# A two-layer kernel on one core: matmuls that nobody reads in TensorE's pauses, one tile taken ahead of the masking, and mix sums moved from GpSimd to VectorE

## What is computed

```python
xa = _ln(x, ln1_w, ln1_b)
sx = concat([state[:, 1:2] - xa[:, :1], xa[:, :-1] - xa[:, 1:]], axis=1)
xxx = tanh((xa + sx * maa_x) @ maa_w1).reshape(b, l, 5, 32)
xxx = einsum('blfd,fde->blfe', xxx, maa_w2)
xm = xa[:, :, None] + sx[:, :, None] * (maa_stack + xxx)      # five mixes: k, w, v, r, g
...
s = a + w_t * s                                                # the scan over 256 tokens
...
og = group_norm(out) * gn_w + gn_b
x1 = x + og * g @ Wo.T
xc = _ln(x1, ln2_w, ln2_b)                                     # then a channel mix with Wfk, Wfr, Wfv
return x1 + sigmoid(xr2 @ Wfr.T) * (square(relu(xk2 @ Wfk.T)) @ Wfv.T)
```

## Time and profile before

| | us |
|---|---|
| median of three runs | 2015.46 |
| lowest, highest | 2014.08, 2019.63 |
| profiled execution, its own time | 2020.89 |
| span of that execution | 2019.2 |
| TensorE busy | 1889.4 (94%) |
| VectorE busy | 1451.3 (72%) |
| ScalarE busy | 870.1 (43%) |
| GpSimd busy | 471.9 (23%) |
| mean granted TensorE clock | 0.973 |

### The profile page before, as it was taken

How to read it: one execution, slowest core, us unless ns; L and a number is a source line. 1 busy time by engine, 2 the same in 40 slices (tenths; PEclk the granted TensorE clock), 3 DMA queues, 4 the chain that set the end, 5 groups by cost and what they waited for, 6 DMA issues and landing times.

```text
span 2019.2 us, 29336 instructions
## 1 busy us (share of the span) xinstructions
PE 1889.4 (94%) x11284; PEld 1289.5 (64%) x11284; DVE 1451.3 (72%) x2477; ACT 870.1 (43%) x2068; POOL 471.9 (23%) x229
## 2 busy tenths in 40 slices
PE   7899999999999999898899999999999999997587
PEld 5576666666666666566666766767766767656343
DVE  3676766667676634257977898889789789789972
ACT  4577666666667746122243342332432432321222
POOL 2333434333333322001211212202211212112000
PEclk9999999999999999999899999999999999998788
DMA  7101000000002012745463654655644645625330
GB/s 215 33 1 38 12 27 27 12 27 12 27 11 79 22 68 65 239 157 170 141 201 119 200 193 151 194 172 166 206 156 157 201 154 167 200 76 173 106 104 32
DMA packets 152787, 227.80 MB, mean 113 GB/s; under 512 B 24184, under 2 KB 72056, under 8 KB 152648
## 3 DMA queue, kind: packets, MB, share of 16 engines
q1 hardware_dynamic: 127272, 205.07, 31.0%
q10 hardware_dynamic: 25376, 20.86, 3.2%
HBM read 183.94 MB, written 41.96 MB: 112 GB/s over the span
## 4 chain that ended last, share of the span: by engine, by line
PE 44%; DVE 6%; DMA 3%; issue 2%; ACT 2%; POOL 2%; ACTq 1%; DVEq 0%; SPq 0%; POOLq 0%
PE b_f_bank L1957 9%; PE b_f_bank L1947 8%; PE b_a_bank L1980 7%; PE b_c_bank L1990 7%; PE b_c_bank L1980 3%; DVE b_ring L2298 2%; PE b_y_bank L2049 2%; PE b_a_bank L2013 2%; DMA b_o<-b_o_all 2%; DVE b_ring L2287 1%; POOL b_mixed L1865 1%; DMA b_o_all<-b_osum 1%; PE b_f_bank L2077 1%; PE b_a_bank L2034 1%; PE b_a_bank L2137 1%
## 5 line engine op out<-in xcount | busy, mean ns | idle before, releaser
L455 POOL TENSOR_TENSOR a_prob<-a_prob,a_rowinv 128x1024 f32<-128x1024 f32 x128 | 242.2, 1893 | 476.5 <-DVE a_rowinv L954 476.5
L1222 ACT ACTIVATE a_prob<-a_score,a_low 128x256 f32<-128x256 f32 x512 | 253.6, 497 | 217.0 <-DVE a_low L946 217.0
L2298 DVE TENSOR_TENSOR_SCAN b_ring<-b_ws,b_ring 128x1028 f32<-128x1028 f32 x128 | 316.7, 2515 | 3.6 <-ACT b_ring L2612 0.7
L1947 PE MATMUL b_f_bank<-k_hT_early,k_w_early 128*128 128x256 f32 x896 | 207.2, 386 | 4.2 <-DVE k_enc_early L2402 2.9
L946 DVE CUSTOM_DVE_ANT_0 a_score<-a_score,a_fill 128x256 f32<-128x256 f32 x512 | 197.2, 449 | 4.6 <-DVE a_score L933 0.2
L1957 PE MATMUL b_f_bank<-k_w_early 128*128 128x512 f32 x448 | 200.3, 597 | 0.0
L1947 PEld LDWEIGHTS b_f_bank<-k_hT_early,k_w_early 128*128 128x128 f32 x896 | 168.4, 191 | 40.4 <-issue 18.6
L2287 DVE TENSOR_TENSOR b_ring<-b_ks,b_vs 128x2048 f32<-128x2048 f32 x64 | 180.5, 2820 | 1.1 <-issue 1.1
L933 DVE SCALAR_TENSOR_TENSOR a_score<-a_S,a_mask 128x1024 f32<-128x1024 f32 x128 | 150.8, 1220 | 42.3 <-PE a_S L654 42.3
L926 DVE TENSOR_SCALAR a_ctxT<-a_O,a_vec 128x256 f32<-128x256 f32 x64 | 31.0, 484 | 202.1 <-PE a_O L685 202.0
L1865 POOL TENSOR_TENSOR b_mixed<-b_mixed,b_xaT 128x1024 f32<-128x1024 f32 x34 | 102.4, 3030 | 254.7 <-DVE b_mixed L2324 254.7
(11 more groups left out here) (203 smaller groups left out, 3008.3 us busy)
## 6 DMA issues: line engine op xcount, KB each, us to landing
k_w_early<-in_w_dram SPq DMA_DIRECT2D x64, 1024.0 KB, 5.5
b_vs<-b_v_all SPq DMA_DIRECT2D x32, 512.0 KB, 5.2
b_shared<-in_Wv_dram SPq DMA_DIRECT2D x8, 1024.0 KB, 6.5
b_shared<-in_Wk_dram SPq DMA_DIRECT2D x8, 1024.0 KB, 5.3
b_shared<-in_Wo_dram SPq DMA_DIRECT2D x8, 1024.0 KB, 6.1
b_shared<-in_Wfk_dram SPq DMA_DIRECT2D x8, 1024.0 KB, 8.5
b_shared<-in_Wfv_dram SPq DMA_DIRECT2D x8, 1024.0 KB, 5.3
b_w_all<-b_wT ACTq DMA_DIRECT2D x8, 514.0 KB, 4.5
```

The costliest lines, as they stand in the source:

```text
L455: nc.gpsimd.tensor_tensor(two, two, inv.to_broadcast([P, 2 * TT, SEQ]), ALU.mult)\
L1222: last = nc.scalar.activation(prob[:, slot, a * SEQ:(a + 1) * SEQ], score[:, j, a * SEQ:(a + 1) * SEQ], ACT.Exp, bias=low[:, head, a:a + 1 ...
L1947: last = nc.tensor.matmul(bank[:, m * SEQ:(m + 1) * SEQ], w1[:, cg, col_:col_ + P], hTf[:, cg, :], start=(cg == 0), stop=(cg == CG - 1))
L2298: last = nc.vector.tensor_tensor_scan(x_, flat(ws[:, :, :]), x_, 0.0, ALU.mult, ALU.add)
```

## The change

It does four things.

1. Ahead of the first transposes TensorE gets 18 matmuls of the identity with itself, written to a part of `S` that the first scores overwrite.
2. In turn `t8` VectorE's `take_ff2(3)` moves ahead of `begin(6)`.
3. The sum of mix 4 moves from GpSimd to VectorE in rounds 3 to 8, and the sums of mixes 0 to 3 in round 9.
4. `keep_clock(n)` issues n matmuls of 128x128 by 128x256 into the third bank of "a", which nothing reads: 8 between `add_rows(s, 6)` and `add_rows(s, 7)` of the last batch, 6 in `group_norm_last` behind the variances, 6 ahead of the turn of `xcT`, 6 ahead of `kk`.

```diff
@@ attention_block, TensorE
+            for _ in range(18):
+                nc.tensor.matmul(S[:, HPG - 1, 0:P], ident[:, :], ident[:, :], start=True, stop=True)
             first = Filler(Turn(-1, ("pre",), ()))
             first.hidden_self(0)
@@ attention_block, VectorE
                 end(5)
-
-                begin(6)
                 if t8:
                     take_ff2(3)
+
+                begin(6)
                 lows(6)
@@ recurrent_block, GpSimd
-                    if s is not None:
+                    if s is not None and f is not None:
                         for f_ in range(4):
                             add_xa(a, f_)
...
-                if a is not None and s is not None and f is not None:
-                    add_xa(a, 4)
@@ recurrent_block, TensorE
+            def keep_clock(n):
+
+                pe.wait_ge(*emptied(LAST, "bonus", 1))
+                for _ in range(n):
+                    nc.tensor.matmul(BANKS["a"][2][:, 0:SEQ], ident[:, :], flat(u_head[:, 0:2, :]), start=True, stop=True)
+
...
                     last.then_inc(full_sem("var"), 1)
+                keep_clock(6)
                 for k in range(2):
                     pe.wait_ge(yg_made.sem, yg_made.at(s, k + 1))
...
+                if d == LAST:
+                    keep_clock(6)
                 if d is not None:
                     pe.wait_ge(xr_made.sem, xr_made.at(d, 1))
                     project_T(d, "kk", loaded("Wfk", d), bv)
...
+                if s == LAST:
+                    keep_clock(8)
                 if s is not None and f is None:
                     add_rows(s, 7)
...
+                if s == LAST:
+                    keep_clock(6)
                 if s is not None:
                     pe.wait_ge(c_h.sem, c_h.at(s, 1))
@@ recurrent_block, VectorE
-                    if s is None:
+                    if s is None or f is None:
                         add_mix(a, 0)
                         add_mix(a, 1)
...
-                    if s is None:
+                    if s is None or f is None:
                         add_mix(a, 2)
                         add_mix(a, 3)
...
-                    if f is None or s is None:
-                        add_mix(a, 4)
+                    add_mix(a, 4)
                     dve.wait_ge(*emptied(a, "r", 1))
```

## The result

| | before | after |
|---|---|---|
| median of four runs of each, on one chip, us | 2015.64 | 1996.91 |
| lowest, highest | 2014.08, 2019.63 | 1995.74, 1998.52 |
| span of the profiled execution | 2019.2 | 1994.4 |
| mean granted TensorE clock | 0.973 | 0.980 |

The ratio is 0.9905 with a 95% interval of [0.9893, 0.9918]: 19.1 us less, between 16.5 and 21.6. The forecast was 1995.4, 20.1 us less. The two profiled executions lie 24.8 us apart, more than the medians; why is a main subject of what follows. Two executions further down, one of 17 of the kernel before (4251.02 us) and one of six of e11 (3955.2), took about twice their time; the medians given include them, the ratios do not.

The account below looks back on a forecast made before the run. TensorE, busy for 94% of the span, was taken as the bound, with time won only where it waits or runs cold. The terms 1.0 + 5.4 + 6.1 + 0.9 + 6.7 = 20.1 us from 2015.5 gave 1995.4, range 1991.0 to 2004.0.

Parts of the forecast that it names:

- Start: First q and k tiles: 18 unread matmuls raise the clock, so k ends at 20.2; -1.0 us, at worst 0.
- before, it ended at 21.15: Start of the kernel: k's first tile, forecast to run from 16.5 to 20.2, was compared with 21.15; -1.0 us.
- Tile: Turn t8: the 3.17 us wait and 2.84 us cold run go, less 0.6 for ScalarE; -5.4, ends 3.2 and 6.0.
- the lateness that the prediction took off with 0.6: Turn t8: ScalarE, whose exponentials follow VectorE's minima, is late next; 0.6 us taken off the gain.
- Fifth sum: Rounds 3 to 8: with mix 4's sum on VectorE, the gate's whole wait goes; -6.1 us, ends 0 and -6.1.
- Four sums in round 9: Round 9: VectorE, the bound there, regains 3.3 us for two sums costing 2.44; -0.9 us.
- The 1.6 more of the prediction: Round 9: up to 1.6 us more if the shorter pause lets the clock stay up in r's projection.
- Last chain: Last chain: unread matmuls hold the clock; 1.1, 3.1, 0.5 and 2.0 won behind four pauses; -6.7 us, ends 0 and -7.5.
- 1: Start and last chain: unread matmuls do not hold the clock, so both give nothing; 2003.1 us, chance 0.10.
- 2: Full rounds: VectorE becomes the bound and the 6.1 us come back at the bonus; 2001.5 us, chance 0.10.
- 3: Turn t8: another bank or ScalarE is late instead, and the 5.4 us are gone; 2000.8 us, chance 0.04.
- 4: Rounds 3 to 8: o += bv waits behind VectorE's sum and product; 7.6 us a round, 2037 us, chance 0.02.

Follow-up runs that it names:

- e11: Changed kernel plus 7 and 11 unread matmuls in the first turn's pauses and 20 and 16 in rounds 9 and 10: 2001.23 us, ratio 0.9917.
- e3: Kernel before with only the sum of mix 4 moved to VectorE in rounds 3 to 8: 2008.1 us, ratio 0.9960.
- e1: Kernel before with only the four groups of unread matmuls (8, 6, 6, 6) in the last chain: 2011.98 us, ratio 0.9973.
- e4: Kernel before with only the four sums of round 9 moved to VectorE: 2015.4 us, ratio 1.0000.
- e2: Kernel before with only take_ff2(3) moved ahead of begin(6) in turn t8: 2013.79 us, ratio 0.9990.
- e7: Changed kernel with 16, 12, 12 and 12 unread matmuls in the last chain instead of 8, 6, 6 and 6: 2007.4 us, ratio 0.9950.
- e9: Kernel before with only the 18 unread matmuls at the start: 2015.39 us, ratio 0.9989.
- e12: The changed kernel once more, unaltered: 1999.78 us, ratio 0.9910 to the kernel before.
- e8: Changed kernel with 7 and 11 more unread matmuls in two pauses of the first turn: 1997.57 us, ratio 0.9903.
- e5: Changed kernel with GpSimd's o += bv held back behind VectorE's k*r product in rounds 3 to 8: 2037.0 us, ratio 1.0094.
- e10: Changed kernel plus 20 unread matmuls ahead of batch 6's output projection and 16 ahead of the last batch's step 4 sums: 1998.84 us, ratio 0.9907.
- e6: Changed kernel with 4, 3, 3 and 3 unread matmuls in the last chain instead of 8, 6, 6 and 6: 2002.36 us, ratio 0.9923.

## Why the prediction was right, point by point

The direction, the size and the range hold: 1996.91 against 1995.4. The terms do not all.

**Start, forecast -1.0: nothing to be seen.** Against the profile before k's first tile ends 1.1 us earlier, as forecast. But the start of that profile was a slow one. Of the 32 records of q's and k's first tiles 12 came at the low clock there, and 13 in e3, but only 7, 7 and 9 in e1, e4 and e2, whose code is the same up to there (first e1, then e3):

```profile
11.38 8.89 PE L552 MATMUL a_G<-k_hT_early,k_w_early 128*128 128x256 f32 x32 [1.32 <-ACT k_hT_early L1176]
```

```profile
11.44 10.01 PE L552 MATMUL a_G<-k_hT_early,k_w_early 128*128 128x256 f32 x32 [1.32 <-ACT k_hT_early L1176]
```

Without the 18 matmuls k's first tile ended at 20.27, 20.16, 20.38, 21.15 and 21.45 us. With them k waits for its weights in each of nine executions; the tile ended between 19.97 and 20.44 in eight, and at 22.48 in e7, where the clock fell behind this wait of 2.06 us. The means lie 0.3 us apart. So the first step that failed is "before, it ended at 21.15", the number of one execution. The second is the sum itself, which carried a lead at 21 us to the end without asking for the next pause. In the profile before the clock survived the pause of 2.93 us ahead of the contexts at 83.39. In the eleven other executions that have this pause it fell there, at the contexts or by the transposes behind them (1.94 us for 16 contexts in e9, 1.97 for 8 transposes in e12); in e8 and e11, where unread matmuls leave 0.5 of it, it did not. So the profile before was the exception, not the 18 matmuls the cause. In the column "first" the executions with the 18 matmuls and this pause have a mean of +0.1, those without the 18 matmuls -0.2.

**Tile, forecast -5.4 (3.2 to 6.0): -4.0, of which about 2 come back.** The wait and the cold records went as forecast: -5.2 in each of the eight traces with the edit against the profile before. (Further on in the turn TensorE waits 1.00 and not 0.21 us for ScalarE in the middle of the 8 transposes of L543: the lateness that the prediction took off with 0.6 is 0.8.) But the five executions without the edit, that one among them, have a mean of -1.2, because behind the same wait of 3.17 the 16 records took 6.46 us only there; they took 5.38 in e1, e4 and e9 and 3.69 in e3. That leaves 4.0, between the ends given. What comes back is a term that the prediction did not have: at the step between the two parts TensorE pauses 2.1 and 0.97 us around 4 small records, and the clock fell there in all eight executions of the changed kernel and its variants (8.83 us for 32 records in after and e5, 10.11 in e12) and in e3, never in the other five. The tile alone (e2) is one of these five. So the tile doesn't bring it on by itself; what does is open, and with it whether these 2 us are the tile's at all. The median of e2, -2.0, allows for 0.2 to 3.8 and so neither for 5.4 nor quite for the 4.0 of the traces, though its own trace gives nothing back at the step: that too is open.

**Fifth sum, forecast -6.1 (ends 0 and -6.1): -8.** e3 measured -8.1 [-5.6, -10.5]; in the traces the eight executions with the edit have a mean of -9.5 in rounds 3 to 8, the five without -1.5. The mechanism is the one forecast: the stretched operation moved from the product to the sum (3.01 us), GpSimd ended at 1161.06, and VectorE was not late in these rounds (TensorE's waits at the bonus are 3.7 us in the six, before as after). Mis-sized was the price of a wait. From the deviations' start to the gate's were 3.11 us (1164.98 to 1168.09) and are 1.83 (1161.11 to 1162.94), so 1.28 and not 1.11: a group that follows without a pause starts before the row of the last one ends. The distance is 3.04 to 3.12 in the unchanged executions (4.17 once, in the earlier trace rows) and 1.81 to 1.83 in the changed ones (2.57 once, in e12). Six rounds make 7.7. The end of -6.1 stood too near; it took the row of waits for all that goes.

**Four sums in round 9, forecast -0.9: -1.07 at its step, not told apart at the end.** From the mixes ahead of the outer product to the sums of L2049 behind it TensorE takes 1.07 us less in each of the nine executions with the edit, and the same as before to 0.01 in the four others without it. On VectorE it is the same: from the first outer product to the next it took 12.39 us (1836.19 to 1848.58), and from the two sums that now stand ahead of it 11.32 (1821.48 to 1832.80). The 1.6 more of the prediction came in five of the nine: TensorE's pause there is 3.01 and not 3.68 us, and r's projection took 7.17; it took 8.7 to 9.2 in the other four, and 8.2 to 8.8 without the edit. But next TensorE waits 10.2 to 13.8 us for VectorE ahead of the output projection of batch 6 (13.65 before, 10.24 after, 13.78 in e12), and when that projection starts differs by 4 us among the executions with the edit and by 2.7 among those without. e4 says 0 with 2.6 either way; in the column "9, 10" the executions with the edit have a mean of -1.9 (e10 and e11 left out), those without -1.3, and single ones lie nearly 6 us apart.

**Last chain, forecast -6.7 (0 to -7.5): -5.4.** Its own steps hold to 0.3 us: output projection 7.13 (7.03 forecast), turn 1.09, `kk` 7.17 (7.24), and `o`, which is loaded as before and now is what TensorE waits for, 0.48 us. Against the profile before the chain is 7.7 shorter. But that execution had the longest chain of all unchanged ones: their mean is 57.5, with 53.9 in e9, where the output projection took 7.13 behind a full pause of 3.52. The six with the full groups have a mean of 52.3 (e5, the seventh, has 51.9). The gain is 5.3, as e1's median says, and lies in what one execution in five gets for nothing.

**The sum.** The terms as the traces show them are 0, 4.0 less 2, 7.9, 0.6 and 5.3, together 16; the single kernels' medians give 2.2, 2.0, 8.1, 0 and 5.4, together 17.7; the whole gives 19.1 [16.5, 21.6] and, repeated, 18.2 [14.5, 21.6]. The 17.7 lie within both intervals; the 16 lie under the first one and 3 us short of its middle, and where those 3 us are is open. That the forecast of 20.1 came so near is in part luck. By the traces the fifth sum was too small by 2 and the other four terms together too large by 6.

**The rivals.** 1 (the unread matmuls don't hold the clock) is refuted: in all seven executions with the full groups `kk` takes 7.17 us and the output projection 7.13; e6 shows that with half of them it falls again. Once it fell ahead of the first deviations (e11, 3.02 us), where VectorE's scan was late and 1.95 us of the pause were left. 2 (VectorE as the bound) is refuted by e3. 3 did not come about in turn t8 itself. 4 costs about what it was said to (e5), with other parts, and its condition is met now and then. In e12 and e10, in the round of the earlier trace rows, the sum started ahead of `o += bv`:

```profile
1440.01 1.23 DVE L2441 TENSOR_TENSOR b_mixed<-b_mixed,b_xaT 128x1024 f32<-128x1024 f32 x1
1440.38 3.05 POOL L1898 TENSOR_TENSOR b_o<-b_o,b_bv 128x1024 f32<-128x1024 f32 x1 [20.69 <-DMA b_o<-b_o_all]
...
1441.16 3.36 DVE L2532 TENSOR_TENSOR b_mixed<-b_kT,b_rT 128x1024 f32<-128x1024 f32 x1
...
1443.49 2.77 PE L1999 MATMUL b_c_bank<-b_o,k_dev_head 128*128 128x256 f32 x8 [2.05 <-POOL b_o L1898]
```

The price was 2.05 us of wait in both, and in e12 0.8 of low clock in the deviations (2.77 for 1.99) and 0.9 in the gate (4.57 for 3.62), not 7.6. The prediction assumed that the product would follow the sum directly. But GpSimd was already waiting and went in between the two, and the product took 3.36. One round of six, in two of the eight executions: it decides nothing.

## What to carry to other kernels

Unread matmuls in a pause are cheap insurance as long as they end before the pause does, and worth it only where TensorE itself is what comes next; where another engine is, the time comes back as a wait. Price a wait by the distance from start to start of the groups around it, not by the wait's row alone. And before an effect of the clock is added to a sum, look at whether the same code shows it in other executions: one trace of the kernel before overstated here what could be won at three places (start, tile, last chain), and hid a fall at a fourth (first turn).

## What the runs showed of the hardware

- The pace of TensorE after equal pauses differs from execution to execution, and so does the number of slow records at the start: 7, 7, 9, 12 and 13 in five executions of the same code. Behind 2.93 us in the first turn the clock stayed up once and fell eleven times; behind 3.17 in turn t8 it stayed up once (e3) and fell four times; behind 3.52 in the last chain it stayed up once (e9) and fell four times; with 2.22 us left it stayed and with 2.24 fell in one and the same execution.
- Of a VectorE and a GpSimd instruction that both read two operands in SBUF, one stood still until the other had ended: 3.01 and 3.36 us for operations that take 1.22. Between two such VectorE instructions GpSimd, already waiting, got its turn in e12; in e5, released at the moment at which the outer product started, it did not, and took 4.49. The Trainium skill (SBUF — State Buffer, § SBUF: two separate sides) says that whichever starts first holds the shared ports for the whole instruction. By that rule both orders agree; that a waiting engine comes between two instructions of the other is shown by e12's rows.
- A matmul of 128x128 by 128x128 in float32, of which nobody reads the result, left two records of 0.12 us each at the high clock (22 in 2.62 us in e8), and one by 128x256 two of 0.23 (16 in 3.72).
